# Unit 0's query low parts moved, the mixing product cut in four, an exact first block of the up projection, and the last tiles' evictions shared anew

## The chip, the cores and the metric

One core of a Trainium2 chip runs the whole program in one launch. The metric is the device time of an execution in microseconds (us). TensorE is called PE here, VectorE DVE, ScalarE ACT, GpSimd POOL, SyncE SP; SP issues all loads and stores of this kernel.

## The reference

`x` has 32 samples of 32 rows of 512 numbers. The block adds two branches to it:

```python
x = x + attn(cond(x, cond_128, ...), Wq, Wk, Wv, Wo, q_norm_w, k_norm_w)
x = x + ffn(cond2(x, cond_128, ...), gate_w, gate_z, gate_s, up_w, up_z, up_s, down_w, down_z, down_s)
...
def cond2(x, embedding, ...):          # 8 experts, one mixed 32x32 matrix a sample
    agg_w = einsum('bk,koi->boi', softmax(...), weight)
    return einsum('boi,bih->boh', agg_w, x) + agg_b[:, :, None]
def dequantize(w, s, z):               # groups of 128 rows; w and z are integers 0 to 15
    return (w - repeat(z, 128)) * repeat(s, 128)
def ffn(x):                            # 512 -> 1792 -> 512
    return (silu(x @ gate_proj) * (x @ up_proj)) @ down_proj
```

Attention has 32 query heads and 8 key/value heads of size 128, over the 32 rows of each sample, with RMS norm on queries and keys, a causal mask and a linear bias. The results are float32, so the kernel splits most operands into a high and a low 16-bit part and adds up three products (high by high, high by low, low by high).

## The kernel before, in words

The program is written by hand, engine by engine; a semaphore stands for each hand-over, and each engine works its list strictly in the order of the code. The work has four parts.

**Start.** A convolution gives the attention's input, the gates of the eight experts are computed, weights and inputs are scaled by powers of two. POOL multiplies the mixing matrices by the gates in one instruction (`mixing_products`, L1792, 2048 numbers a partition); DVE sums that product over the experts (`mixing_sums`, L1450).

**Attention** runs in 16 units, two halves of the tokens for each of 8 key/value heads. In unit 0, which has no unit in front of it to fill its waits, PE projects the queries, turns them (`transpose_q`, L676), turns the keys (`transpose_k`, L683), projects keys and values of unit 1 and computes the scores. ACT evicts a turned query block to `qhi` (L1086), DVE computes the low part `qlo` (`queries_low`, L1473). `transpose_k` waits for the second `qlo`, since it writes the same PSUM bank. In DVE's list the scaling of the output weights (`scale_wo`, L1364, 2048 numbers a partition, in SBUF) stands in front of the first two `queries_low`. Each later unit also prepares a part of the FFN's weights: `up_ints` (DVE, L1525) takes the zeros off, `up_scaled` (POOL) multiplies by the scales, `up_high` (ACT) and `up_low` (DVE, L1529) split the product into `uphi` and `uplo`, all four blocks of 128 rows at once. Gate and down weights stay exact integers (`gint`, `dints`), and their scales are applied when a product is evicted.

**FFN** has 28 tiles, 14 slices of the inner size for each half of the tokens. For tile n PE runs `gate(n)` (4 blocks, 2 matmuls each, L852 and L853), the first two blocks of `down(n-2)`, `up(n)` (4 blocks, 3 matmuls each, L539 to L541), and the last two blocks of `down(n-2)` (L888, L889; 2 matmuls each). ACT and DVE evict the gate blocks by turns into `whole` and `part` (L1213, L1689), POOL adds the two (`add_part`, L1905), ACT applies silu (L1218), DVE multiplies by the up product (`hidden`, L1695), ACT and POOL split the result into `hThi` and `hTlo` (L1224, L1911). DVE adds down blocks 0, 2 and 3 to `acc` (L1704); block 1 goes through ACT (L1236) and POOL (L1921). `whole` and `part` have two buffers, so ACT's eviction of gate block 0 of tile n waits for `hTlo` of tile n-2.

The first two tiles lie beside the last unit of the attention. DVE computes the scales of a half in `mix_scales` (L1676, L1677), between two steps that PE waits for.

**End.** After tile 27 PE runs `down(26)` and `down(27)`, then `turn_last` turns the second half's result back (L915), DVE adds it to `x` in four steps (`result`, L1717), and SP stores (L527).

Of the kernel before, what the change touches and what calls it, by code (L numbers as in the profile page):

```python
# [86 lines left out]
def build(nc, x_in, xt_in, mask_in, fs_in, cond_in, cw_in, conv_in, wq_in, wkv_in, wo_in, w0_in, w1_in, w2_in, b2_in, mix_in, vec_in,  # L87
          gu_w_in, gu_z_in, gu_s_in, up_s_in, dn_w_in, dn_z_in, dn_s_in, const_in, sel_in, out):
    ctx = ExitStack()
    with ctx:  # L90
# [83 lines left out]
        uplo = sb("uplo", [P, IC, KC, P], F16)  # L174
# [35 lines left out]
        rest = sb("rest", [P, DM - 2 * IC * KC - IC * KC - 2 * HQ - 10], F32, att)  # L210
# [31 lines left out]
        between = sb("between", [P, 7 * DM + 40], F32, ffn)  # L242
# [103 lines left out]
        d_gint = sem("d_gint")  # L346
        d_usub = sem("d_usub")
# [11 lines left out]
        d_fscl = sem("d_fscl")  # L359
        t_fT = sem("t_fT")  # L360
# [6 lines left out]
        a_silu = sem("a_silu")  # L367
        t_u = sem("t_u")
        d_h = sem("d_h")
# [6 lines left out]
        a_dn = sem("a_dn")  # L376
        p_acc = sem("p_acc")
# [26 lines left out]

        def turned_bank(half, c):

            return side if half else (PA[0], PA[1], PC[2], PC[3])[c]
# [9 lines left out]
        def down_bank(n, c):  # L417

            return bank[c] if n == TILES - 1 else PC[c % 2]
# [27 lines left out]
        def _(sp):  # L447
# [77 lines left out]
            for q in range(NQ):  # L525
                sp.wait_ge(d_res, q + 1)
                sp.dma_start(out[:, q, :], x[:, q, :]).then_inc(l_out, 16)  # L527
# [4 lines left out]
        def _(pe):  # L532
# [306 lines left out]
            def gate(n):  # L839
# [3 lines left out]
                for g in range(KC):  # L843
# [6 lines left out]
                    if g == 0 and n in (1, 2):  # L850
                        pe.wait_ge(d_h, n)
# [4 lines left out]
            def up(n):  # L856
# [3 lines left out]
                if n < 2:  # L860
                    pe.wait_ge(a_g, 2 * n + 1)
                elif n == 2:
                    pe.wait_ge(d_y, HQ * UNITS)
                else:
                    pe.wait_ge(d_h, n)
                split_product(up_bank(n)[:, :], [(uphi[:, i, c, :], uplo[:, i, c, :], fThi[:, c, tokens(half)],
                                                  fTlo[:, c, tokens(half)]) for c in range(KC)],
                              True, True).then_inc(t_u, 1)

            def down(n, blocks=range(KC)):  # L870
                last = n == TILES - 1
                pe.wait_ge(a_dtr, n + 1)
                if last:
                    pe.wait_ge(d_hlo, 1)
                else:
                    pe.wait_ge(p_hlo, n + 1)
                for c in blocks:
                    if last:
                        pe.wait_ge(d_g if c % 2 else a_g, 2 * TILES - 1 + c // 2)
                    elif c >= 2:  # L880
# [5 lines left out]
                    ints = dtr[:, n % 2, P * c:P * c + P]  # L886
                    o = down_bank(n, c)
                    mm(o[:, :], ints, hThi[:, n % (LAG + 1), :], start=True, stop=False)  # L888
                    mm(o[:, :], ints, hTlo[:, n % (LAG + 1), :], start=False, stop=True).then_inc(t_dn, 1)  # L889
# [13 lines left out]
            def turn_last():  # L903
# [3 lines left out]
                pe.wait_ge(d_res, HQ)  # L907
                pe.wait_ge(d_h, TILES)
                for c in (0, 2, 3, 1):
# [4 lines left out]
                    for t in range(HQ):  # L914
                        last = nc.tensor.transpose(PC[t][:, P * c:P * c + P], acc[:, 1, c, P * t:P * t + P], ident)  # L915
                        if c == 1:
                            last.then_inc(t_yT, 1)
# [41 lines left out]
            for n in range(TILES - LAG, TILES):  # L959
                down(n)  # L960
# [4 lines left out]
        def _(act):  # L965
# [108 lines left out]
            def up_high(i):  # L1074
                act.wait_ge(p_umul, i + 1)
                A(uphi[:, i, :, :], raw[:, 1, :].bitcast(F32).rearrange("p (c n) -> p c n", c=KC), ACT.Copy,
# [126 lines left out]
            def scaled(n, g):  # L1203
                half, i = divmod(n, IC)
                act.wait_ge(t_g, KC * n + g + 1)
                if i == 0 and g == 0:
                    act.wait_ge(d_fscl, half + 1)
# [11 lines left out]

            def hidden_high(n):  # L1220
                act.wait_ge(d_h, n + 1)
# [28 lines left out]
            outputs_high(UNITS - 1)  # L1250
            gate(0)
            hidden_high(0)
            mix_input(4)
            scaled(1, 0)
            scaled(1, 2)
            mix_input(5)
            gate(1)
            hidden_high(1)
            mix_input(6)
            act.wait_ge(d_dint, IC)  # L1260
# [3 lines left out]
            for n in range(2, TILES):  # L1264
# [16 lines left out]
                down_ints(n - 1)  # L1281
                gate(n)
# [3 lines left out]
            down_scaled(TILES - 1)  # L1286
# [3 lines left out]
        def _(dve):  # L1290
# [157 lines left out]
            def mixing_sums(h):  # L1448
                dve.wait_ge(p_mixp, 1)
# [73 lines left out]
            def up_ints(i):  # L1523
                dve.wait_ge(l_up, 48 * i + 48)
                V.tensor_tensor(raw[:, 1, :].bitcast(F32), raw[:, 1, :], zeros[:, 1, :], ALU.subtract).then_inc(d_usub, 1)  # L1525

            def up_low(i):
                dve.wait_ge(a_uphi, i + 1)
                V.scalar_tensor_tensor(uplo[:, i, :, :], raw[:, 1, :].bitcast(F32).rearrange("p (c n) -> p c n", c=KC),  # L1529
                                       upk[:, 0:1], uphi[:, i, :, :], ALU.mult, ALU.subtract).then_inc(d_uplo, 1)  # L1530
# [160 lines left out]
            def hidden(n):  # L1691
                dve.wait_ge(a_silu, n + 1)
                dve.wait_ge(t_u, n + 1)
# [311 lines left out]
```

## Time and profile before

| what | us |
| --- | --- |
| median of 3 runs (732.04 to 732.96) | 732.92 |
| the profiled execution | 738.87 |
| its span, first to last instruction | 737.1 |

The profile describes the one execution of 738.87 us. "Busy" is the time in which an engine had an instruction under way. Matmuls are pipelined: a record of one 512-column matmul is about 0.38 us long, while the next begins 0.216 us after it. The granted clock is 1.00 at the full 2.4 GHz and 0.50 at 1.2 GHz.

### The profile page before, as it was taken

To read this page: it belongs to the slowest core of one execution; us is meant where nothing else is said; L and a number is where in the kernel's file an instruction comes from. 1 tells how busy PE (TensorE), PEld (TensorE's weight loads), DVE (VectorE), ACT (ScalarE), POOL (GpSimd) and SP (SyncE) were. 2 spreads that over 40 slices of the span, in tenths; PEclk is the share of its full clock that TensorE was granted. 3 is DMA by queue.
4 is the path that set the end of the run, shared out by engine and by line. 5 is a ranking of instruction groups with operands and counts; after the bars stand their busy time and mean duration, and the time that the engine had idled before them with its cause. 6 is when DMAs were issued, how large, how long until landed. Compare 5 with 4: busy or idle time off the path is not lost.

```text
span 737.1 us, 14750 instructions
## 1 busy us (share of the span) xinstructions
PE 719.0 (98%) x5350; PEld 433.6 (59%) x5350; DVE 503.6 (68%) x764; ACT 438.2 (59%) x1293; POOL 420.6 (57%) x349
## 2 busy tenths in 40 slices
PE   9997999999999999999999999999899999999996
PEld 8755555656656566565665656656545555555554
DVE  5977777677666757666776775574655776666666
ACT  1475574845757576495575757647555665545553
POOL 0473974853766484485476648448334556646663
PEclk9998999999999999999999999999999999999999
DMA  8410242342331323234233121220000000010001
GB/s 267 189 40 1 102 144 73 116 157 71 114 128 57 117 93 103 71 114 153 75 113 129 57 93 64 73 72 30 1 1 1 0 1 2 0 44 16 0 1 58
DMA packets 21738, 54.20 MB, mean 74 GB/s; under 512 B 3744, under 2 KB 4288, under 8 KB 19520
## 3 DMA queue, kind: packets, MB, share of 16 engines
q1 hardware_dynamic: 21696, 53.67, 21.6%
q8 instruction: 22, 0.36, 0.2%
q14 instruction: 20, 0.16, 0.1%
HBM read 51.57 MB, written 2.10 MB: 73 GB/s over the span
## 4 chain that ended last, share of the span: by engine, by line
PE 87%; DVE 5%; POOL 5%; ACT 2%; issue 1%; DMA 1%; SPq 0%; DVEq 0%; ACTq 0%; POOLq 0%
PE bank L539 21%; PE bank L540 20%; PE bank L541 20%; PE bank L676 4%; PE bank L888 3%; PE bank L889 3%; PE bank L852 3%; PE bank L853 3%; PE bank L591 2%; PE bank L718 1%; POOL wqlo L1803 1%; PE bank L683 1%; PE bank L703 1%; PE bank L693 1%; PE bank L692 1%
## 5 line engine op out<-in xcount | busy, mean ns | idle before, releaser
L539 PE MATMUL bank<-wohi,oThi 128*128 128x512 f16 x256 | 97.2, 380 | 1.7 <-DVE oTlo L1507 1.6
L539 PE MATMUL bank<-wqhi,cThi 128*128 128x512 f16 x256 | 97.1, 379 | 1.2 <-POOL wqlo L1803 0.6
L540 PE MATMUL bank<-wolo,oThi 128*128 128x512 f16 x256 | 97.1, 379 | 0.0
L541 PE MATMUL bank<-wohi,oTlo 128*128 128x512 f16 x256 | 97.1, 379 | 0.0
L540 PE MATMUL bank<-wqlo,cThi 128*128 128x512 f16 x256 | 97.1, 379 | 0.0
L541 PE MATMUL bank<-wqhi,cTlo 128*128 128x512 f16 x256 | 97.1, 379 | 0.0
L1820 POOL TENSOR_TENSOR qinv<-qms,neghalf 128x8 f32<-128x8 f32 x32 | 52.7, 1646 | 46.4 <-ACT qms L1028 46.4
L1020 ACT ACTIVATE qsq<-qraw 128x128 f32<-128x128 f32 x256 | 75.8, 299 | 4.7
L1515 DVE SCALAR_TENSOR_TENSOR x<-bank,ysc,x 128x512 f32<-128x512 f32 x64 | 48.0, 750 | 42.2 <-PE bank L541 41.6
L1813 POOL TENSOR_TENSOR wolo<-wor,wohi 128x512 f16<-128x512 f32 x32 | 36.3, 1156 | 70.1 <-ACT wohi L991 70.1
L1911 POOL TENSOR_TENSOR hTlo<-whole,hThi 128x512 fp32r<-128x512 f32 x27 | 34.6, 1282 | 71.1 <-ACT hThi L1224 71.1
L1827 POOL TENSOR_TENSOR qn<-qraw,qinv 128x512 f32<-128x512 f32 x64 | 68.8, 1094 | 4.2 <-POOL qinv L1820 3.2
L539 PE MATMUL bank<-wkvhi,cThi 128*128 128x256 f16 x256 | 70.4, 275 | 0.0
L540 PE MATMUL bank<-wkvlo,cThi 128*128 128x256 f16 x256 | 70.3, 275 | 0.0
L541 PE MATMUL bank<-wkvhi,cTlo 128*128 128x256 f16 x256 | 70.2, 274 | 0.0
L1086 ACT ACTIVATE qhi<-bank 128x512 f16<-128x512 f32 x64 | 36.1, 590 | 46.7 <-PE bank L676 46.0
L1704 DVE SCALAR_TENSOR_TENSOR acc<-bank,dscl,acc 128x512 f32<-128x512 f32 x78 | 55.6, 742 | 0.5 <-PE bank L889 0.5
L888 PE MATMUL bank<-hThi,dtr 128*128 128x512 f32 x112 | 54.5, 486 | 1.0 <-ACT dtr L1229 0.7
L1803 POOL TENSOR_TENSOR wqlo<-wqr,wqhi 128x512 f16<-128x512 f32 x32 | 37.9, 1215 | 26.4 <-ACT wqhi L977 26.4
L1473 DVE TENSOR_TENSOR qlo<-bank,qhi 128x512 f16<-128x512 f32 x64 | 42.6, 686 | 12.2 <-ACT qhi L1086 12.2
L1507 DVE SCALAR_TENSOR_TENSOR oTlo<-bank,oThi 128x512 f16<-128x512 f32 x64 | 39.7, 684 | 15.2 <-ACT oThi L1112 15.2
L1695 DVE SCALAR_TENSOR_TENSOR whole<-bank,hc,whole 128x512 f32<-128x512 f32 x28 | 21.0, 751 | 40.8 <-PE bank L541 36.7
(194 smaller groups left out, 1884.5 us busy)
## 6 DMA issues: line engine op xcount, KB each, us to landing
wqr<-in_wq SPq DMA_DIRECT2D x8, 1024.0 KB, 4.8
wor<-in_wo SPq DMA_DIRECT2D x8, 1024.0 KB, 4.9
raw<-in_gu_w SPq DMA_DIRECT2D x28, 256.0 KB, 2.8
zeros<-in_gu_z SPq DMA_DIRECT2D x28, 256.0 KB, 3.6
wkvr<-in_wkv SPq DMA_DIRECT2D x8, 512.0 KB, 4.1
srow<-in_up_s SPq DMA_DIRECT2D x14, 256.0 KB, 4.1
raw<-in_dn_w SPq DMA_DIRECT2D x14, 256.0 KB, 3.2
zeros<-in_dn_z SPq DMA_DIRECT2D x14, 256.0 KB, 4.4
```

Source lines behind the costliest of these rows:

```text
L539: mm(o, ahi, bhi, start=start and k == 0, stop=False)
L540: mm(o, ahi, blo, start=False, stop=False)
L541: last = mm(o, alo, bhi, start=False, stop=stop and k == n - 1)
L888: mm(o[:, :], ints, hThi[:, n % (LAG + 1), :], start=True, stop=False)
L1020: A(qsq[:, t % 2, g, :], qraw[:, t, g, :], ACT.Square, accum_out=qss[:, t, g:g + 1]).then_inc(a_qss, 1)
L1473: V.tensor_tensor(qlo[:, BQ * t:BQ * t + BQ, :, :].rearrange("p b g s -> p g b s"), query_bank(u, t)[:, :].rearrange("p (g b s) -> p g b s ...
L1507: V.scalar_tensor_tensor(oTlo[:, :, :, b, :], PC[b][:, :].rearrange("p (t g s) -> p t g s", t=HQ, g=G), O_DOWN, oThi[:, :, :, b, :], ALU.m ...
L1515: V.scalar_tensor_tensor(x[:, q, :], PC[t][:, :], ysc[:, half:half + 1], x[:, q, :], ALU.mult, ALU.add).then_inc(d_y, 1)
L1704: V.scalar_tensor_tensor(o, down_bank(n, c)[:, :], dscl[:, i, c:c + 1], o, ALU.mult, ALU.add).then_inc(d_dn, 1)
L1803: Q.tensor_tensor(wqlo[:, c, :], wqr[:, c, :], wqhi[:, c, :], ALU.subtract).then_inc(p_wq, 1)
L1820: Q.tensor_tensor(qinv[:, pair, :], qms[:, pair, :], neghalf[:, pair, :], ALU.pow).then_inc(p_qpow, 1)
L1827: Q.tensor_tensor(qn[:, t, :, :], qraw[:, t, :, :], qinv[:, t, :, None].broadcast_to([P, G, HD]), ALU.mult).then_inc(p_qn, 1)
```

## The change

Four edits. (1) In DVE's list for unit 0 the first two `queries_low` stand in front of `scale_wo`, and the maximum over the second key/value weights stands behind `queries_low(0, 3)`. (2) `mixing_products` is four instructions of a quarter each. (3) Block 0 of the up weights stays integers: its two matmuls make a product of their own (PE list: one matmul less a tile), in bank PA[1] for tiles 0 and 1 and PA[0] after; ACT evicts it with its scale into a new tile `exact` (`up_exact`); DVE adds the other blocks' product to it (`up_sum`, in the place of `hidden`), POOL multiplies by the silu result (`hidden`, new on POOL; on DVE for the last tile), and POOL's and ACT's lists are put in another order. The preparation of the up weights works on three blocks; block 0 is one DVE subtraction. `mix_scales` has one instruction more, and its second call goes to ACT (`later_scales`). (4) At the end `down(26)` and `down(27)` use banks of their own, the order of DVE's list changes, and one of the four final additions goes through ACT and POOL, with a store issued by ACT.

```diff
@@ DVE, unit 0
             score_scale()
-            scale_wo()
             queries_low(0, 0)
             queries_low(0, 1)
-            link(weight_max(M_KV, wkvr, l_wkv, 1))
+            scale_wo()
             keys_low(0)
             queries_low(0, 2)
             queries_low(0, 3)
+            link(weight_max(M_KV, wkvr, l_wkv, 1))
             out_scale()
@@ POOL
-                Q.tensor_tensor(mixp[:, :, :, :], ..., ALU.mult).then_inc(p_mixp, 1)
+                for q in range(0, NQ, 2):
+                    Q.tensor_tensor(mixp[:, q:q + 2, :, :], ..., ALU.mult).then_inc(p_mixp, 1)
@@ PE, up(n)
                 if n < 2:
-                    pe.wait_ge(a_g, 2 * n + 1)
-                elif n == 2:
+                    pe.wait_ge(d_g, 2 * n + 1)
+                pe.wait_ge(a_g, 2 * n + 1)
+                o = exact_bank(n)[:, :]
+                mm(o, uphi[:, i, 0, :], fThi[:, 0, tokens(half)], start=True, stop=False)
+                mm(o, uphi[:, i, 0, :], fTlo[:, 0, tokens(half)], start=False, stop=True).then_inc(t_ue, 1)
+                if n == 2:
                     pe.wait_ge(d_y, HQ * UNITS)
-                else:
-                    pe.wait_ge(d_h, n)
-                split_product(up_bank(n)[:, :], [... for c in range(KC)],
+                elif n > 2:
+                    pe.wait_ge(d_us, n)
+                split_product(up_bank(n)[:, :], [... for c in range(1, KC)],
                               True, True).then_inc(t_u, 1)
@@ PE, last tiles
+            def last_downs():
+                n = TILES - 2
+                pe.wait_ge(a_dtr, n + 1)
+                pe.wait_ge(p_hlo, n + 1)
+                pe.wait_ge(d_res, HQ)
+                down_block(n, 0)
+                pe.wait_ge(d_us, TILES)
+                down_block(n, 1)
...
+                n = TILES - 1
+                pe.wait_ge(a_dtr, n + 1)
+                pe.wait_ge(d_hlo, 1)
+                down_block(n, 1)
...
@@ ACT
+            def up_exact(n):
+                half, i = divmod(n, IC)
+                act.wait_ge(t_ue, n + 1)
+                if n >= 2:
+                    act.wait_ge(p_h, n - 1)
+                A(exact[:, n % 2, :], exact_bank(n)[:, :], ACT.Copy, scale=uscl[:, half, i:i + 1]).then_inc(a_u, 1)
@@ ACT, tile n of the loop
-                if n > 2:
-                    hidden_high(n - 1)
                 scaled(n, 2)
+                hidden_high(n - 1)
                 if n >= LAG:
                     down_scaled(n - LAG)
+                up_exact(n)
@@ ACT, end
-            down_scaled(TILES - 1)
+            A(dprod[:, 1, :], down_bank(TILES - 1, 1)[:, :], ACT.Copy, ...).then_inc(a_dn, 1)
+            act.wait_ge(t_yT, HQ + 1)
+            A(fnat[:, 0, :], last_bank(0)[:, :], ACT.Copy).then_inc(a_yT, 1)
+            act.wait_ge(p_res, 1)
+            act.dma_start(out[:, HQ, :], x[:, HQ, :]).then_inc(l_out, 16)
@@ DVE
             def mix_scales(half):
...
+                link(V.tensor_scalar(uscl[:, half, :], gus[:, 1, :, 0], finv[:, column], None, ALU.mult))
...
+            def up_sum(n):
+                dve.wait_ge(a_u, n + 1)
+                dve.wait_ge(t_u, n + 1)
+                u = exact[:, n % 2, :]
+                V.scalar_tensor_tensor(u, up_bank(n)[:, :], hc[:, n // IC:n // IC + 1], u, ALU.mult,
+                                       ALU.add).then_inc(d_us, 1)
...
-                hidden(n)
+                up_sum(n)
+                if n == TILES - 1:
+                    last_hidden()
                 if n >= LAG:
                     down_added_to(n - LAG, 2)
-                if n == 7:
-                    mix_scales(1)
+            hidden_low(TILES - 1)
             down_added_to(TILES - 3, 3)
             down_added_to(TILES - 2, 0)
-            hidden_low(TILES - 1)
@@ POOL, tile n of the loop
                 if n > LAG:
-                    hidden_low(n - 1)
+                    hidden(n - 1)
+                    add_down(n - 1 - LAG)
                 add_part(n)
-                add_down(n - LAG)
+                hidden_low(n - 1)
+            pool.wait_ge(d_hlo, 1)
+            add_down(TILES - 1 - LAG)
             add_down(TILES - 2)
             add_down(TILES - 1)
+            pool.wait_ge(a_yT, 1)
+            Q.tensor_tensor(x[:, HQ, :], fnat[:, 0, :], x[:, HQ, :], ALU.add).then_inc(p_res, 1)
```

## Rows read from the trace of the kernel before

**Rows 1.** The page: the span, and PE's busy time, share and instructions

```profile
span 737.1 us, 14750 instructions
PE 719.0 (98%) x5350; PEld 433.6 (59%) x5350; DVE 503.6 (68%) x764; ACT 438.2 (59%) x1293; POOL 420.6 (57%) x349
```

**Rows 2.** Windows: stretch, length, busy us of each engine, granted clock, DMA

```profile
58.70:63.20 4.50, 4.49 (x21) 3.85 (x22) 3.38 (x6) 2.95 (x11) 0.00 (x0) 0.50 0.00 0
...
107.00:524.00 417.00, 416.89 (x3540) 252.99 (x3538) 278.40 (x416) 261.95 (x907) 251.96 (x216) 1.00 0.28 92
```

**Rows 3.** Waits of PE in 0 to 107 us: total us, times, longest

```profile
PE bank L683 <- DVE qlo L1473: 4.7, 1, 4.7
```

**Rows 4.** Timeline of DVE, units 0 and 12: start, us, line, operation, tiles

```profile
41.14 0.94 DVE L1444 TENSOR_TENSOR mixb<-le,vec 128x64 f32<-128x64 f32 x1
51.76 5.61 DVE L1364 TENSOR_SCALAR wor<-wor,wup 128x2048 f32<-128x2048 f32 x1
57.29 1.27 DVE L1473 TENSOR_TENSOR qlo<-bank,qhi 128x512 f16<-128x512 f32 x2
58.48 1.20 DVE L1336 TENSOR_REDUCE mx<-wkvr 128x1 f32<-128x1024 f32 x1
65.81 0.42 DVE L1462 SCALAR_TENSOR_TENSOR vlo<-bank,vhi 128x256 f16<-128x256 f32 x1 [2.57 <-ACT vhi L1044]
...
430.45 1.29 DVE L1364 TENSOR_SCALAR wor<-wor,wup 128x2048 f32<-128x2048 f32 x1
```

**Rows 5.** Timeline of POOL, unit 0

```profile
40.92 2.09 POOL L1827 TENSOR_TENSOR qn<-qraw,qinv 128x512 f32<-128x512 f32 x2
51.78 4.50 POOL L1792 TENSOR_TENSOR mixp<-mixw,le 128x2048 f32<-128x2048 f32 x1
```

**Rows 6.** Timelines of ACT and PE, unit 0

```profile
51.87 1.08 ACT L1086 ACTIVATE qhi<-bank 128x512 f16<-128x512 f32 x2 [0.72 <-DVE wn L1435]
53.59 0.38 PE L541 MATMUL bank<-wqhi,cTlo 128*128 128x512 f16 x1
61.29 0.42 PE L539 MATMUL bank<-wkvhi,cThi 128*128 128x256 f16 x1
```

**Rows 7.** The chain of work that ended last: start, us, what

```profile
67.79 1.05 POOL sc L1841
101.56 4.50 DMA srow<-in_up_s
540.87 0.39 PE bank L539
```

**Rows 8.** Timeline of PE over one tile of the FFN

```profile
687.05 0.39 PE L852 MATMUL bank<-fThi,gint 128*128 128x512 f16 x1
689.73 0.39 PE L539 MATMUL bank<-fThi,uphi 128*128 128x512 f16 x1
693.26 0.39 PE L852 MATMUL bank<-fThi,gint 128*128 128x512 f16 x1
```

**Rows 9.** Window over the same tile

```profile
687.05:693.26 6.21, 6.21 (x29) 3.31 (x29) 4.21 (x7) 3.62 (x6) 3.78 (x3) 1.00 0.00 1
```

**Rows 10.** Timelines of ACT and POOL over the same tile

```profile
687.70 0.69 ACT L1213 ACTIVATE whole<-bank,gscl 128x512 f32<-128x512 f32 x1 [1.58 <-PE bank L853]
691.71 0.63 ACT L1218 ACTIVATE whole<-whole 128x512 f32<-128x512 f32 x1 [0.59 <-POOL whole L1905]
...
690.41 1.27 POOL L1905 TENSOR_TENSOR whole<-whole,part 128x512 f32<-128x512 f32 x1 [0.15 <-DVE part L1689]
```

**Rows 11.** Timeline of DVE before the first tiles

```profile
533.38 0.25 DVE L1677 TENSOR_SCALAR gscl<-gus,finv 128x56 f32<-128x56 f32 x1
```

**Rows 12.** Timelines of PE and DVE at the end

```profile
718.14 0.39 PE L852 MATMUL bank<-fThi,gint 128*128 128x512 f16 x1
...
727.58 3.38 DVE L1704 SCALAR_TENSOR_TENSOR acc<-bank,dscl,acc 128x512 f32<-128x512 f32 x5 [0.23 <-PE bank L889]
731.82 2.48 DVE L1717 TENSOR_TENSOR x<-bank,x 128x512 f32<-128x512 f32 x4 [0.86 <-PE bank L915]
```

More of the change, by code:

```diff
@@ L241, in build @@
         hTlo = sb("hTlo", [P, LAG + 1, HT], F32R, ffn)
-        between = sb("between", [P, 7 * DM + 40], F32, ffn)
+        exact = sb("exact", [P, 2, HT], F32, ffn)
+        between = sb("between", [P, 5 * DM + 40], F32, ffn)
         dtr = sb("dtr", [P, 2, DM], F32R, ffn)
@@ L376, in build @@
         a_dn = sem("a_dn")
+        a_yT = sem("a_yT")
+        p_res = sem("p_res")
         p_acc = sem("p_acc")
@@ L860, in up, with down_block, down @@
                 if n < 2:
-                    pe.wait_ge(a_g, 2 * n + 1)
-                elif n == 2:
+                    pe.wait_ge(d_g, 2 * n + 1)
[4 more added lines that the diff above has]
+                if n == 2:
                     pe.wait_ge(d_y, HQ * UNITS)
-                else:
-                    pe.wait_ge(d_h, n)
-                split_product(up_bank(n)[:, :], [(uphi[:, i, c, :], uplo[:, i, c, :], fThi[:, c, tokens(half)],
-                                                  fTlo[:, c, tokens(half)]) for c in range(KC)],
+                elif n > 2:
+                    pe.wait_ge(d_us, n)
+                split_product(up_bank(n)[:, :], [(uphi[:, i, c, :], uplo[:, i, c - 1, :], fThi[:, c, tokens(half)],
+                                                  fTlo[:, c, tokens(half)]) for c in range(1, KC)],
                               True, True).then_inc(t_u, 1)
-            def down(n, blocks=range(KC)):
-                last = n == TILES - 1
+            def down_block(n, c):
+                ints = dtr[:, n % 2, P * c:P * c + P]
+                o = down_bank(n, c)[:, :]
+                mm(o, ints, hThi[:, n % (LAG + 1), :], start=True, stop=False)
+                mm(o, ints, hTlo[:, n % (LAG + 1), :], start=False, stop=True).then_inc(t_dn, 1)
+            def down(n, blocks):
                 pe.wait_ge(a_dtr, n + 1)
[L873 to L876, printed above, removed]
+                pe.wait_ge(p_hlo, n + 1)
                 for c in blocks:
-                    if last:
-                        pe.wait_ge(d_g if c % 2 else a_g, 2 * TILES - 1 + c // 2)
-                    elif c >= 2:
+                    if c >= 2:
                         pe.wait_ge(a_dn if c == 3 else d_dn, n + 1 if c == 3 else down_added(n, 0))
@@ L885, in down @@
                         pe.wait_ge(d_y, HQ * (UNITS - 1) + c + 1)
[L886 to L889, printed above, removed]
+                    down_block(n, c)
+            def last_downs():
+                n = TILES - 2
+                pe.wait_ge(a_dtr, n + 1)
+                pe.wait_ge(p_hlo, n + 1)
+                pe.wait_ge(d_res, HQ)
+                down_block(n, 0)
+                pe.wait_ge(d_us, TILES)
+                down_block(n, 1)
+                pe.wait_ge(a_g, 2 * TILES)
+                down_block(n, 2)
+                pe.wait_ge(d_g, 2 * TILES)
+                down_block(n, 3)
+                n = TILES - 1
+                pe.wait_ge(a_dtr, n + 1)
+                pe.wait_ge(d_hlo, 1)
+                down_block(n, 1)
+                pe.wait_ge(a_u, TILES)
+                down_block(n, 0)
+                pe.wait_ge(d_dn, down_added(n - 2, 3))
+                down_block(n, 2)
+                down_block(n, 3)
             def turn_back(half, q):
@@ L958, in _ @@
                     turn_back(0, 2 * n - 2 * IC - 2 * LAG + 1)
-            for n in range(TILES - LAG, TILES):
-                down(n)
+            last_downs()
             turn_last()
@@ L1734, in _ @@
             outputs_low(UNITS - 1)
-            hidden(0)
+            up_sum(0)
             up_low(IC - 1)
@@ L1740, in _ @@
             add_outputs(UNITS - 1, 1, 1)
-            hidden(1)
+            up_sum(1)
             add_outputs(UNITS - 1, 1, 2)
@@ L1779, in _ @@
                 down_added_to(TILES - 1, c)
-            for q in range(HQ, NQ):
+            for q in range(HQ + 1, NQ):
                 result(q)
@@ L1905, in add_part, with hidden @@
                 Q.tensor_tensor(whole[:, n % 2, :], whole[:, n % 2, :], part[:, n % 2, :], ALU.add).then_inc(p_whole, 1)
+            def hidden(n):
+                pool.wait_ge(d_us, n + 1)
+                pool.wait_ge(a_silu, n + 1)
+                Q.tensor_tensor(whole[:, n % 2, :], whole[:, n % 2, :], exact[:, n % 2, :], ALU.mult).then_inc(p_h, 1)
             def hidden_low(n):
@@ L1927, in _ @@
             add_part(0)
+            mix_low(4)
+            hidden(0)
+            mix_low(5)
+            add_part(1)
             hidden_low(0)
-            mix_low(4)
-            add_part(1)
-            mix_low(5)
-            hidden_low(1)
             mix_low(6)
+            hidden(1)
             mix_low(7)
```

91 lines of the change are left out of this document (61 added, 30 removed).

## The prediction

> **What bounds the kernel now.** I read the page first: PE is busy for 719.0 of 737.1 us [rows 1]. So a gain must come from fewer matmuls or from the few places where PE waits or runs slowly. The windows by stage say where these are. From 107 to 524 us, units 2 to 15, PE is busy for 416.89 of 417.00 us [rows 2]: nothing done to other engines there can gain. The table of waits names one long wait of PE ahead of 107 us, 4.7 us of the key transposes for `qlo` [rows 3]. A window behind it adds that from 58.70 to 63.20 us the granted clock was 0.50, the 1.2 GHz level, after that idle time [rows 2]. In the FFN one tile takes 693.26 - 687.05 = 6.21 us of unbroken matmuls [rows 8], while DVE is busy for 4.21, ACT for 3.62 and POOL for 3.78 us of it [rows 9]: PE sets the pace. The end is a serial stretch of evictions [rows 12].
>
> **Unit 0.** The wait comes from DVE's list. `scale_wo` began at 51.76 and took 5.61 us, against 1.29 us for the same instruction in unit 12; it ended 1.1 us after POOL's 4.50 us product, which ran from 51.78 to 56.28 [rows 4, 5]. So DVE stood behind POOL, and both `qlo` stood behind DVE. After the change the two `qhi` are there at 52.4 and 52.95 (from 51.87, 0.54 us each [rows 6]), and the two `qlo`, which read PSUM, take 0.6 us each [rows 4]: done at 53.7. PE's last matmul of the projection ends at 53.59 + 0.38 = 53.97 [rows 6], so the transposes start at once, 4.7 us earlier. At 61.29 the key and value matmuls began at the low clock [rows 6]. Without the idle time I expect no drop, since PE's work in front of it ran at full clock; 4.5 us of half-clock work becomes 2.25, a second gain of 2.25 us. That makes 6.95 for PE.
>
> DVE must keep up. `scale_wo` waits for a POOL instruction to end. With pieces of 4.50 / 4 = 1.13 us the next end is at 54.0, so it runs to 55.3. Then `klo` and two `qlo` of about 0.65 us to 57.3, the maximum moved behind them, 1.20 us [rows 4], to 58.5, two small scalings of some 0.45 us together, and `vlo` starts at 58.95 instead of 65.81 [rows 4]: 6.8 us earlier. DVE, not PE, sets the shift, and POOL's step at 67.79, which follows from `vlo` over the scores, moves with it [rows 7]. From there to 107 us the chain runs through POOL, a load of 4.50 us issued after POOL's step, and PE [rows 7]; each is released by the one in front, so all shift alike. **Gain 6.8 us**; bounds 4.5 (DVE does not get in between the pieces, below) and 6.95.
>
> That DVE gets in rests on `mixb`: two POOL instructions followed each other from 40.92 for 2.09 us; `mixb`, issued at 41.14, ended at 42.08, just behind the first of them [rows 4, 5]. The waiting engine was let in at the boundary. The delayed pieces of the product cost nothing: they end at 57.6, POOL has nothing to do before its step at 67.79 - 6.8 = 61.0 [rows 7], and DVE reads them later still.
>
> **Up weights in units 2 to 15 and the head of the FFN.** One more DVE instruction and shorter DVE, POOL and ACT work per slice: nothing, hidden behind PE (416.89 of 417.00 busy [rows 2]). If the cover were gone the small DVE instruction would cost about 0.1 us each time, 14 times.
>
> **FFN tiles.** PE runs 28 matmuls less, 29 - 1 per tile. From 687.05 to 689.73 lie twelve matmuls, 0.223 us each; the f16 ones alone step by 0.216 (the section on the profile has it), and I take that. In tile 0 it gains nothing, since PE then waits for `oTlo` until 540.87 [rows 7]. Tiles 1 to 27: 27 x 0.216 = **5.8 us**, if no new wait appears. Bounds 0 and 6.05.
>
> So I walk through the new tile of 6.0 us, from its first gate matmul, with durations of [rows 9, 10]. ACT: gate block 0 from 0.65 (687.70 - 687.05), block 2 to 2.15, `hThi` to 2.75, down block 1 to 3.45, the new `up_exact` (0.69 us long, 0.59 from start to start) to 4.05, `dtr` to 4.6, silu to 5.2 (before: 691.71 + 0.63, that is 5.3). In sum 3.62 + 0.6 = 4.2 of 6.0 us. DVE: no instruction more, 4.21. POOL: four instead of three instructions of 1.27 us, 5.1 of 6.0 us: the new product waits for `up_sum` of the tile before at 0.1 and ends at 1.35, `add_down` 2.6, `add_part`, which needs both DVE gate evictions, from 3.0 to 4.25, `hTlo` to 5.5. PE's own new wait, gate block 0 evicted before the exact block enters its bank, ends at 1.25, needed at 2.7. The next gate block 0 waits for `up_exact`, 4.05, needed at 6.0. `hTlo` at 5.5 is needed by ACT at 6.65. Every wait ends over 0.6 us early.
>
> **Scales ahead of the first tiles.** `uscl` is one more linked DVE instruction between two low parts that PE needs; its neighbour takes 0.25 [rows 11]. PE's step at 540.87 [rows 7] comes **0.2 us later**; bounds 0 and 0.3. In half 1 the same work moves to ACT, beside PE's matmuls: nothing, or some 0.8 us once if tile 7 had no slack.
>
> **The end.** Measured from tile 27's first gate matmul, 718.14 [rows 12], the span ends after 18.96 us. The new banks let `down(26)` follow at once, so `hThi` and `hTlo` of tile 27 set `down(27)` at about 8.1 us. DVE still adds seven blocks behind that, at 3.38 / 5 = 0.68 us [rows 12]: to 12.9 us, where the last one ended at 730.96, 12.8, before. The last steps shrink: four additions in 2.48 us [rows 12] become three, 0.6 us less, with the fourth over ACT (0.69) and POOL (1.27 [rows 10]) in parallel, 2.0 us against 1.9. The new store from ACT's queue starts no later than SP's last. Together 0.6 us less, of which 0.2 is tile 27's matmul, counted above: **gain 0.4 us**; bounds -1.0 (POOL's branch and its store end last) and 1.5.
>
> **Sum.** 6.8 + 5.8 - 0.2 + 0.4 = 12.8 us. Against the profiled execution, 738.87 us, this gives 726.1. The median of the runs shown is 732.92, 0.8% lower; no term scales enough for that to matter, so I predict 732.92 - 12.8 = **720.1 us**.
>
> **The rivals.**
> *DVE is not let in between the pieces.* POOL's four pieces follow each other, and `scale_wo` waits until about 56.4. Then `vlo` starts 58.95 + 2.3 = 61.25, the gain in unit 0 is 4.5, and the time is 722.4. `mixb` speaks against it, though it is one case with another DVE instruction. The Trainium skill, page "SBUF — State Buffer", section "SBUF: two separate sides", says that DVE and GpSimd share a port pair as an exclusive lock: whoever starts first holds it for the whole instruction and the other fully blocks. By that rule the 5.61 us [rows 4] are explained, but nothing promises the waiting side the next turn, and the time would be this rival's 722.4.
> *The clock still falls.* If the low clock comes anyway, 2.25 us are lost: 722.4 too. Against it: the idle time in front of it is gone.
> *The matmul saved is waited away.* A hand-over in the new order ends last in each tile and the tile stays at 6.21: 5.8 less gain, 725.9. The slack of 0.6 us on POOL is the thinnest.
> *Slower: the ring over two buffers of `whole`.* From gate block 0's eviction at 0.65 to `hTlo` of the same tile at 6.0 + 5.5 is 10.85 us, and it must fit in two tiles. The other gains are 7.0 us; spread over 26 tiles that is 0.27, so it decides from a tile of 6.48, a ring of 12.96. If each of POOL's four steps were held up by a DVE instruction of 0.74 us, the ring would be 13.8, a tile 6.9, and the time 732.92 - 7.0 + 26 x 0.69 = 744. Against it: DVE's FFN instructions read PSUM, and beside them POOL's 1.27 us do not vary.
> *A gain that isn't there.* Unit 0's shift is taken back before 107 us by something that I didn't see, and the tiles gain nothing: about 732.5.
>
> **Chances.** Forecast 0.70; either of the two at 722.4 0.13; 725.9 0.10; slower 0.03; no gain 0.04, of which half counts as small gains. A measurement of this kernel can tell 0.2%, 1.5 us, from no change: faster 0.95, same 0.02, slower 0.03. The low end takes the upper bounds of unit 0 and the end, 720.1 - 0.15 - 1.1 and some tenths for an execution's spread: 718.3. The high end takes in 722.4 with the lower bound of the end: 723.6. Outside lie 725.9 and what is worse, 0.17.
>
> **What would show it.** In the changed profile: `scale_wo` about 1.3 us long from 54; no wait of 4.7 us at `transpose_k`, clock 1.00 from 54 to 66; `vlo` at 59; the first PE-bound stretch from 100 us; a tile of 6.0 us in the FFN, with POOL busy for 5.1; the span's end 18.4 us after tile 27's first matmul. The forecast is wrong if a tile takes over 6.1 us, or if the clock is below 1 after 54 us.

## The result, and the profile after

| | before | after |
|---|---|---|
| median of the timed runs | 732.48 us (731.84 to 732.96) | 727.98 us (727.12 to 728.39, 4 runs) |
| the profiled execution | 738.87 us | 728.39 us |
| its span | 737.1 us | 725.1 us |
| its mean granted clock | 0.994 | 0.999 |

The ratio of the times is 0.9938, 95% interval 0.9920 to 0.9955: faster by 4.5 us, where 12.8 were forecast, and 4.4 us above the high end of the range. The two spans differ by 12.0 us. So the traces show nearly the gain that was predicted, and the runs do not. That is the question of this case.

The page and the windows of the kernel after; the first window is unit 0 behind the evictions of the queries, the second one FFN tile (stretch, length, then busy us of PE, PEld, DVE, ACT, POOL with instructions, the granted clock, DMA):

```profile
span 725.1 us, 14838 instructions
PE 709.9 (98%) x5322; PEld 429.3 (59%) x5322; DVE 497.4 (69%) x777; ACT 453.3 (63%) x1325; POOL 452.4 (62%) x380
...
53.00:66.00 13.00, 12.50 (x121) 8.43 (x120) 11.30 (x17) 10.43 (x39) 10.03 (x9) 1.00 0.00 1
700.23:706.23 6.00, 6.00 (x28) 3.21 (x28) 4.24 (x7) 4.19 (x7) 5.05 (x4) 1.00 0.00 0
```

PE has 28 matmuls less than in [rows 1]. The tile is 6.00 us long against the 6.21 of [rows 9], with all of it PE's, and unit 0 runs at full clock. The same stretch of the kernel before:

```profile
53.00:66.00 13.00, 8.26 (x88) 6.74 (x87) 9.31 (x10) 5.91 (x26) 3.28 (x1) 0.74 0.00 0
```

88 matmuls instead of 121, at a mean clock of 0.74. Unit 0 of the kernel after, timelines of DVE and POOL:

```profile
51.02 0.16 DVE L1505 TENSOR_TENSOR wn<-wcol 128x1 f32<-128x1 f32 x1
51.92 1.29 DVE L1543 TENSOR_TENSOR qlo<-bank,qhi 128x512 f16<-128x512 f32 x2 [0.73 <-ACT qhi L1132]
53.12 1.28 DVE L1434 TENSOR_SCALAR wor<-wor,wup 128x2048 f32<-128x2048 f32 x1
59.08 0.42 DVE L1532 SCALAR_TENSOR_TENSOR vlo<-bank,vhi 128x256 f16<-128x256 f32 x1
...
51.02 1.07 POOL L1916 TENSOR_TENSOR kn<-kraw,kinv 128x512 f32<-128x512 f32 x1
52.06 5.94 POOL L1872 TENSOR_TENSOR mixp<-mixw,le 128x512 f32<-128x512 f32 x4
```

`scale_wo` (`wor`) fits between two pieces of the product: 1.28 us instead of 5.61, and the four pieces take 5.94 where the whole took 4.50 [rows 4, 5]. `vlo` starts at 59.08, was 65.81. PE's wait of 4.7 us for `qlo` is gone. The seam before the first tiles and the last tile, from PE's and DVE's timelines:

```profile
526.70 0.24 DVE L1749 TENSOR_SCALAR uscl<-gus,finv 128x14 f32<-128x14 f32 x1
534.46 0.39 PE L561 MATMUL bank<-wohi,oThi 128*128 128x512 f16 x1 [0.74 <-DVE oTlo L1577]
706.23 0.39 PE L876 MATMUL bank<-fThi,gint 128*128 128x512 f16 x1
712.36 0.69 DVE L1775 TENSOR_TENSOR whole<-whole,exact 128x512 f32<-128x512 f32 x1
714.36 4.70 DVE L1783 SCALAR_TENSOR_TENSOR acc<-bank,dscl,acc 128x512 f32<-128x512 f32 x7
719.80 1.88 DVE L1796 TENSOR_TENSOR x<-bank,x 128x512 f32<-128x512 f32 x3 [0.74 <-PE bank L962]
```

Read against [rows 7, 12]: PE's step in front of the tiles moves from 540.87 to 534.46, 6.4 us. Tile 27 begins at 706.23 instead of 718.14, 11.9 us; so the FFN gave 5.5. Behind it the end takes 725.1 - 706.23 = 18.87 us against 18.96.

### The profile page after: what moved, and what is told of

It reads as the page before. It is cut to its first block, busy times and chain, and to the rows that moved or that the text cites. A ratio compares the mean times of both kernels' runs of the same rounds, so it can differ in the third digit from the quotient of the medians.

```text
span 725.1 us, 14838 instructions
## 1 busy us (share of the span) xinstructions
PE 709.9 (98%) x5322; PEld 429.3 (59%) x5322; DVE 497.4 (69%) x777; ACT 453.3 (63%) x1325; POOL 452.4 (62%) x380
## 4 chain that ended last, share of the span: by engine, by line
PE 86%; POOL 5%; DVE 4%; DMA 2%; issue 1%; SPq 1%; ACT 1%; DVEq 0%; POOLq 0%
PE bank L561 20%; PE bank L563 20%; PE bank L562 20%; PE bank L698 3%; PE bank L901 3%; PE bank L902 3%; PE bank L876 3%; PE bank L877 3%; PE bank L740 2%; POOL wqlo L1883 1%; DMA xT<-in_xt 1%; PE bank L888 1%; PE bank L705 1%; PE bank L889 1%; PE bank L725 1%
## 5 line engine op out<-in xcount | busy, mean ns | idle before, releaser
L1543 DVE TENSOR_TENSOR qlo<-bank,qhi 128x512 f16<-128x512 f32 x64 | 42.4, 685 | 12.8 <-ACT qhi L1132 12.8
L1986 POOL TENSOR_TENSOR whole<-whole,part 128x512 f32<-128x512 f32 x28 | 35.5, 1270 | 24.9 <-DVE part L1762 24.9
L1066 ACT ACTIVATION_READ_ACCUMULATOR qsq<-qraw 128x1 f32 x256 | 48.4, 189 | 0.0
```

The lines of the kernel that those rows point to most:

```text
L1066: A(qsq[:, t % 2, g, :], qraw[:, t, g, :], ACT.Square, accum_out=qss[:, t, g:g + 1]).then_inc(a_qss, 1)
L1543: V.tensor_tensor(qlo[:, BQ * t:BQ * t + BQ, :, :].rearrange("p b g s -> p g b s"), query_bank(u, t)[:, :].rearrange("p (g b s) -> p g b s ...
```

## The experiments

All times are medians of timed runs, beside runs of the kernel before on the same chip; "traced" means the profiled execution of that kernel.

### Is the profiled execution of before like its timed runs?

**e1_before_again** is the kernel before, unchanged; **e7_after_again** the kernel after, unchanged.

> The kernel of before, unchanged, timed and profiled once more. Theory A (an order that is decided anew in each execution): whether DVE's scaling of the output weights or POOL's mixing product gets going first in unit 0 differs from execution to execution; the timed runs at 732.5 us are those where DVE is first, the profiled one at 738.87 us one where it lost. Then a new profile shows either a scaling of 1.3 us and a span of 729 to 731 us, or one of 5.6 us and 737 us, and the timed median stays at 732.5. Theory B (the stall is in every execution, and the profiled execution was slower for another reason): the scaling takes 5.6 us again and the span is 737 us, while the timed runs stay at 732.5.

Measured: the traced execution took 738.83 us, and the eleven others of this label 732.06 to 732.86; the 27 runs beside it 731.71 to 733.80, median 732.6. The spans of the others are 730.2 to 731.0 us, the traced one's 736.9. So one program has two times, 6.2 us apart, and both of its two traces so far caught the longer one. DVE and POOL in the traced execution:

```profile
51.26 1.05 DVE L1435 TENSOR_TENSOR wn<-wcol 128x1 f32<-128x1 f32 x1
52.23 5.61 DVE L1364 TENSOR_SCALAR wor<-wor,wup 128x2048 f32<-128x2048 f32 x1
...
51.25 1.04 POOL L1836 TENSOR_TENSOR kn<-kraw,kinv 128x512 f32<-128x512 f32 x1
52.25 4.51 POOL L1792 TENSOR_TENSOR mixp<-mixw,le 128x2048 f32<-128x2048 f32 x1
```

> The changed kernel, unchanged, timed beside the others. It is 5.7 us below before in span and was 4.5 below in time. If what lies outside the span belongs to the change (a store on ACT's queue): time minus span is 3.3 again and the time 728.0. If it belonged to those runs alone: time minus span is 2.1, as in the kernel without the unit 0 edits, and the time 727.4.

Measured: 727.49 us (726.96 to 728.57), ratio 0.9927 [0.9913, 0.9940]. All nine timed runs of the kernel after so far lie between 726.96 and 728.57: it has one time.

### Each part of the change by itself

**e2_unit0_alone**: the kernel before with the new order in unit 0 and the product in four pieces.

```diff
-                dve.wait_ge(p_mixp, 1)
+                dve.wait_ge(p_mixp, 2 * h + 2)
...
-            scale_wo()
             queries_low(0, 0)
             queries_low(0, 1)
-            link(weight_max(M_KV, wkvr, l_wkv, 1))
+            scale_wo()
             keys_low(0)
             queries_low(0, 2)
             queries_low(0, 3)
+            link(weight_max(M_KV, wkvr, l_wkv, 1))
...
+                for q in range(0, NQ, 2):
+                    Q.tensor_tensor(mixp[:, q:q + 2, :, :], ...)
```

> Only the moved query low parts and the mixing product in four pieces, on the kernel of before. Theory A: the timed runs of before mostly lack the stall, so the time is 732.5 us, within 1 us; the profile shows no wait of 4.7 us and a span of about 730 us. Theory B: the edit takes 6.8 us off every execution, 725.7 us.

Measured: 732.35 us, ratio 0.9998 [0.9989, 1.0007]. **e3_unit0_undone** takes the same lines out of the kernel after.

> The changed kernel with the two unit 0 edits undone. Theory A: the time is that of the changed kernel, 728.0 us within 1 us, in runs where DVE is first; the exact block and the end alone give the 4.5 us. Theory B: 728.0 + 6.8 = 734.8 us.

Measured: 727.54 us, ratio 0.9932 [0.9919, 0.9946], against 727.49 with them (e7). Unit 0's edits are worth 0.0 to 0.3 us in timed runs, from both sides. The trace of e3 is the first to show the old list without the stall:

```profile
51.25 0.16 DVE L1505 TENSOR_TENSOR wn<-wcol 128x1 f32<-128x1 f32 x1
51.33 2.07 DVE L1434 TENSOR_SCALAR wor<-wor,wup 128x2048 f32<-128x2048 f32 x1
...
51.26 1.06 POOL L1915 TENSOR_TENSOR kn<-kraw,kinv 128x512 f32<-128x512 f32 x1
52.28 5.51 POOL L1871 TENSOR_TENSOR mixp<-mixw,le 128x2048 f32<-128x2048 f32 x1
```

This is what to compare with e1, line by line. Here `wn`, a product of one number per partition, takes 0.16 us; `scale_wo` is then issued while `kn` runs, gets in behind it and is done at 53.40; POOL's product pays, 5.51 instead of 4.50. In e1 `wn` takes 1.05 us and ends with `kn`. `scale_wo` and the product are then recorded 0.02 us apart, at 52.23 and 52.25; that the product was in front is read from the durations, 5.61 against 4.51. The first trace of before has the same pair, at which I had not looked:

```profile
50.78 1.05 DVE L1435 TENSOR_TENSOR wn<-wcol 128x1 f32<-128x1 f32 x1
...
50.78 1.04 POOL L1836 TENSOR_TENSOR kn<-kraw,kinv 128x512 f32<-128x512 f32 x1
```

What gives `wn` 0.16 or 1.05 us is finer than these hundredths. The trace of e2 has the starts of e1, and the short `wn`:

```profile
51.26 0.16 DVE L1435 TENSOR_TENSOR wn<-wcol 128x1 f32<-128x1 f32 x1
...
51.25 1.07 POOL L1837 TENSOR_TENSOR kn<-kraw,kinv 128x512 f32<-128x512 f32 x1
```

In nanoseconds, over all traces in which nothing was put in front of `wn`, its record starts from 9 ahead of `kn`'s to 4 behind it in the ten with the short `wn`, and 5 to 7 behind it in the three with the long one (before, e1 and e14). So "who comes first" below is inferred from this order: `kn`'s record may start up to 4 ns ahead and `wn` is still not held up.

**e8_end_undone** keeps the exact block and takes the end back: the old banks, the order of the last low part and additions, the last eviction by DVE, all stores by SP.

```diff
-            hidden_low(TILES - 1)
             down_added_to(TILES - 3, 3)
             down_added_to(TILES - 2, 0)
+            hidden_low(TILES - 1)
...
-            for q in range(HQ + 1, NQ):
+            for q in range(HQ, NQ):
                 result(q)
...
-            pool.wait_ge(d_hlo, 1)
             add_down(TILES - 1 - LAG)
```

> The changed kernel with the end put back: banks, orders of DVE and PE, four final additions on DVE, all stores by SP. By the prediction's term the new end is worth 0.4 us, so 0.4 above the changed kernel. By the traces (the stretch from tile 27's first matmul to the end was 18.96 before and is 18.87 now, one matmul of 0.22 less included): 0 to 0.2 us below the changed kernel in span, and 0.3 more below it in time if the ACT store costs that outside the span.

Measured: 729.50 us (728.81 to 730.38), ratio 0.9950 [0.9937, 0.9964]: 3.3 us for the exact block, and 2.0 for the new end. DVE, POOL and PE of e8 in the last tile, and the windows around the wait:

```profile
712.74 1.33 DVE L1755 TENSOR_TENSOR whole<-whole,exact 128x512 f32<-128x512 f32 x1
...
712.23 1.30 POOL L1987 TENSOR_TENSOR acc<-acc,dprod 128x512 f32<-128x512 f32 x1
...
714.88 0.77 PE L897 MATMUL bank<-hThi,dtr 128*128 128x512 f32 x1 [2.10 <-DVE acc L1763]
...
712.80:714.85 2.05, 0.00 (x0) 0.00 (x0) 2.05 (x3) 1.26 (x2) 0.73 (x1) 1.00 0.00 0
714.85:718.20 3.35, 3.32 (x7) 2.16 (x8) 1.91 (x4) 0.69 (x1) 0.47 (x1) 0.50 0.00 0
```

The exact block turns the last tile's product from an instruction that reads a bank into one with two inputs in SBUF. DVE's list has one instruction more there: the sum into `exact` takes the 0.75 us that `hidden` took before, and the product comes on top. With the old end the product meets POOL's addition and takes 1.33 us instead of 0.69; PE waits 2.1 us, where it waited 0.72 at the same place of the kernel before, and the granted clock behind that idle time is 0.50, the 1.2 GHz level, for 3.35 us. From tile 27's first matmul (706.63) to the end it is 21.1 us. The new end makes POOL wait for `d_hlo` and fills PE's gap with `down(26)`: 18.87. So the new end removes what the exact block would cost there.

### What decides between the two times of before?

My theory after e1 to e3 was: whoever comes first of `wn` and `kn`. The rival was that the moment at which `scale_wo` is issued decides.

**e4_scale_late**: three linked memsets of one number ahead of `scale_wo`, to bring it behind `kn`'s end.

```diff
             score_scale()
+            for _ in range(3):
+                link(V.memset(rowmax[:, :], 0.0))
             scale_wo()
```

> The kernel of before with three tiny DVE memsets in front of the scaling in unit 0, so that POOL's mixing product is always under way first. Theory A: every execution has the stall: 738 to 739 us, 6 us above before, scaling of 5 to 5.6 us in the profile, granted clock 0.5 for some us behind it. Theory B: before has it already, so the time stays at 732.5 us.

Measured: 732.81 us, ratio 1.0002 [0.9993, 1.0011]; the expected stall did not come, also not in the trace:

```profile
51.94 1.68 DVE L1364 TENSOR_SCALAR wor<-wor,wup 128x2048 f32<-128x2048 f32 x1
...
52.50 5.51 POOL L1794 TENSOR_TENSOR mixp<-mixw,le 128x2048 f32<-128x2048 f32 x1
```

The memsets were too short: `scale_wo` was issued at 51.94, `kn` ended at 52.54. A delay of 0.6 us inside `kn` costs nothing. That it is the side of `kn`'s end that counts is tested by the runs that follow.

**e5_stall_forced** puts DVE behind the product for certain: a first piece of an eighth, DVE waits for it, then come seven eighths. **e6_stall_forced_moved** adds the new order of DVE's list, with the wait still ahead of `scale_wo`.

```diff
             score_scale()
+            dve.wait_ge(p_mixp, 1)
             scale_wo()
...
+                for part_q in (slice(0, 1), slice(1, NQ)):
```

> The kernel of before, with the mixing product in two pieces (one eighth, then seven eighths) and DVE's scaling in unit 0 waiting for the first piece, so that POOL's long piece (about 3.9 us) is always under way before the scaling can start. Theory A (the stall is absent from the timed runs of before; its price is what the profiled execution showed): 738.8 us, 6.2 above before, in all timed runs, with the scaling over 4 us long and the clock at 0.5 behind the wait. Theory C (the stall is in the timed runs too, or costs nothing outside a profile): 732.6 us.

Measured: 739.42 us (738.96 to 740.26), ratio 1.0090 [1.0077, 1.0104]. The stall costs 6.6 us in timed runs too. In the trace `wn` took 0.16 us and `scale_wo`, issued behind the first piece, 4.97. So theory and rival are two links of one chain: the stall comes when `scale_wo` is issued too late to be ahead of the product, and a `wn` that is held up is what makes it late in the kernel before.

> The same forced order, with the query low parts moved in front of the scaling as in the change, the product still in two pieces. If moving alone is enough: 732.6 us. By the prediction's rival, where DVE is not let in between the pieces: the key low part waits for the scaling, about 57.5 us, and some 2 us of the stall stay: 734.5 us.

Measured: 735.92 us, ratio 1.0034 [1.0021, 1.0048]. PE's waits of `qlo` in e5 and in e6:

```profile
PE bank L683 <- DVE qlo L1473: 4.9, 1, 4.9
```

```profile
PE bank L691 <- DVE qlo L1473: 1.7, 1, 1.7
```

The order alone recovers 3.5 of 6.6 us: `scale_wo` is still held, 4.68 us, and now the last two `qlo`, for which the scores wait, stand behind it. That the pieces recover the rest is not shown by a pair of runs that differ in the pieces alone; e10 and e14, with both edits, have the order that stalls and no such wait.

**e9_wn_behind_kn** and **e10_after_wn_behind_kn** force the order of `wn` and `kn` in the kernels before and after.

```diff
+                dve.wait_ge(p_kn, 1)
                 V.tensor_tensor(wn[:, :], wcol[:, 0:1], wcol[:, 3:4], ALU.mult).then_inc(d_wn, 1)
```

> The kernel of before, where one tiny DVE instruction (wn, one number a partition) waits for POOL's kn, which normally starts within some 10 ns of it; nothing else is changed. Theory A, with its detail: which of the two is first decides all. With wn first, DVE's scaling is already waiting when kn ends and gets in ahead of the mixing product; with kn first, the product is under way when the scaling is issued. So 738.8 to 739.4 us in all timed runs. Rival: the order of these two doesn't matter, the product has to be issued early for another reason: 732.6 us.

Measured: 739.56 us (738.87 to 740.07), ratio 1.0091 [1.0076, 1.0107]. DVE of e9:

```profile
51.82 4.37 DVE L1436 TENSOR_TENSOR wn<-wcol 128x1 f32<-128x1 f32 x1 [1.18 <-POOL kn L1837]
56.12 1.28 DVE L1364 TENSOR_SCALAR wor<-wor,wup 128x2048 f32<-128x2048 f32 x1
```

One product of 128 numbers took 4.37 us beside POOL's 4.50, and `scale_wo` behind it its usual 1.28.

> The same added wait in the changed kernel. If the two unit 0 edits take the decision out of chance, the time stays at 727.5 us, at most 0.5 above; so the change would be worth 12 us in this order of the two, and 5 in the other.

Measured: 729.58 us (728.20 to 730.14), ratio 0.9951 [0.9935, 0.9967]. That is 2.1 above e7, where I expected at most 0.5. The spans, mostly 726.1 to 726.5 us against 724.8 to 725.4 in e7, account for 1.2 of it: PE waits 1.2 us of a `qlo`, as `wn` had to wait for the first piece of the product, and `scale_wo` took 1.65 us between two others. The rest lies outside the span, where three of these six runs have over 3 us (see "Outside the span" below). In this order the change is worth 739.56 - 729.58 = 10.0 us.

**e13_wn_a_little_later** touches nothing but a moment: one linked memset of one number, 0.06 us, ahead of `wn`.

```diff
+                link(V.memset(rowmax[:, :], 0.0))
                 V.tensor_tensor(wn[:, :], wcol[:, 0:1], wcol[:, 3:4], ALU.mult).then_inc(d_wn, 1)
```

> The kernel of before with one DVE memset of one number a partition, some 0.1 to 0.15 us, in front of wn, and no added wait on POOL. Theory A: wn and kn start within 10 ns of each other, so this is enough to put wn behind kn: 738.8 to 739.5 us in all timed runs. Rival: the two are further apart in the timed runs than in a trace, and the order holds: 732.7 us.

Measured: 738.79 us, all twelve runs from 738.10 to 739.74; ratio 1.0056 [1.0027, 1.0084]. DVE and POOL:

```profile
51.06 0.93 DVE L1436 TENSOR_TENSOR wn<-wcol 128x1 f32<-128x1 f32 x1
51.91 5.61 DVE L1364 TENSOR_SCALAR wor<-wor,wup 128x2048 f32<-128x2048 f32 x1
...
50.93 1.04 POOL L1837 TENSOR_TENSOR kn<-kraw,kinv 128x512 f32<-128x512 f32 x1
51.93 4.50 POOL L1793 TENSOR_TENSOR mixp<-mixw,le 128x2048 f32<-128x2048 f32 x1
```

With a memset of 0.06 us, which puts the start of `wn` 0.13 us behind that of `kn`, the kernel before is 6 us slower in every run. The ratio is smaller than the 1.0083 of the medians (738.79 over 732.74), and its interval wide, because of the 18 runs of before beside it 5 took 738.4 to 739.9 us, with spans of 736.6 to 738.1, and one 735.84: here, without being traced, the unchanged kernel fell on the long side as well. Of the 62 timed runs of it before this job none had; one, also at 735.84, lay between.

### What is left to gain at the end and at the seam

**e11_store_by_sp**: the kernel after, with the last store issued by SP instead of ACT.

```diff
+            sp.wait_ge(p_res, 1)
+            sp.dma_start(out[:, HQ, :], x[:, HQ, :]).then_inc(l_out, 16)
...
-            act.wait_ge(p_res, 1)
-            act.dma_start(out[:, HQ, :], x[:, HQ, :]).then_inc(l_out, 16)
```

> The changed kernel, with the last store issued by SP behind the three others instead of by ACT. Time minus span was 1.8 in all runs of before and of kernels without that store, 2.1 to 3.5 with it. If ACT's store is the cause: 1.8 again, the span the same or 0.3 longer (the issue comes behind three others), 727.2 us. If it is not: 2.1 or more stays, 727.5 us or above.

Measured: 727.12 us, ratio 0.9924 [0.9907, 0.9941], beside 727.49 of e7 in another job: 0.4 less, not distinct. Time minus span was 1.95 to 2.2 us in five runs and 3.4 in one, so it did not go back to 1.8.

**e12_scales_later** (e11 with the scales behind PE's needs, `up_scales` last) and **e14_scales_in_gap** (all three together in DVE's gap); in both ACT waits for the scales ahead of its first `up_exact`:

```diff
             turned_low(0, 0)
-            mix_scales(0)
             turned_low(0, 1)
...
             turned_low(0, 3)
+            mix_scales(0)
             scaled(0, 1)
             scaled(0, 3)
+            up_scales()
```

> As the kernel with the store by SP, and the three small DVE scalings ahead of the first tiles moved: the gate scales behind the fourth low part, the other two behind the second gate eviction. If the chain through the low parts sets PE's next step there, as the prediction took it, 0.5 to 0.7 us less: 726.6 us. If other waits hold it: 727.2 us.

Measured: 728.03 us, ratio 0.9940 [0.9924, 0.9956]: 0.9 slower than e11. DVE and PE of e12:

```profile
531.62 1.22 DVE L1754 TENSOR_SCALAR uscl<-gus,finv 128x14 f32<-128x14 f32 x1
...
535.28 0.39 PE L563 MATMUL bank<-wohi,oThi 128*128 128x512 f16 x1 [1.84 <-DVE oTlo L1579]
```

> As the kernel with the scales moved, but the other two small scalings directly behind the gate scales, where DVE sat idle for 0.9 us, and ahead of POOL's first addition, which held one of them up for a microsecond. If the scales' place in DVE's list is what the 0.3 us ahead of the first tiles hang on: the step of PE that waited at 534.4 comes 0.4 to 0.6 us earlier and the time is 0.5 below the kernel with the store by SP, 726.6 us. If not: 727.1 us.

Measured: 726.79 us (725.63 to 728.12), ratio 0.9901 [0.9864, 0.9938]; the runs of before beside it include the long ones. The same two places in e14:

```profile
528.94 0.23 DVE L1754 TENSOR_SCALAR uscl<-gus,finv 128x14 f32<-128x14 f32 x1
...
533.52 0.39 PE L563 MATMUL bank<-wohi,oThi 128*128 128x512 f16 x1 [0.47 <-DVE oTlo L1579]
```

In e12, behind `scaled(0, 3)`, the 14 numbers of `uscl` met a POOL addition and took 1.22 us for 0.24, and PE's step came at 535.28; in the gap, 533.52. The whole trace of e14 runs early, though: 0.49 us of its 0.94 ahead of the kernel after are there before this seam. Counted from DVE's `sc` in front of it, PE's step comes after 14.16 us in the kernel after, 15.09 in e12 and 13.71 in e14, so the place gives 0.45, as expected. This is the lowest median of the study, 0.7 below e7, but across jobs and within the spread of single runs.

The trace of e14 also settles what e10 could only force. By itself it fell into the order that stalls the kernel before, and its span is the shortest of all traces, 724.1 us:

```profile
50.55 1.05 DVE L1507 TENSOR_TENSOR wn<-wcol 128x1 f32<-128x1 f32 x1
53.46 1.66 DVE L1436 TENSOR_SCALAR wor<-wor,wup 128x2048 f32<-128x2048 f32 x1
```

`wn` was held up for 0.9 us and `scale_wo` for 0.4, no wait of PE for `qlo` appeared, and the granted clock stayed at 1.00 behind it. As far as this one execution shows, with both unit 0 edits it no longer matters which order comes about.

## Why the prediction was wrong

**The failed step is "Sum".** I saw that the median of the runs, 732.92, was 0.8% below the profiled execution, 738.87, and wrote that no term scales enough for that to matter. Nothing scales: the 6 us are one event. The 4.7 us wait of [rows 3] and the low clock of [rows 2] are in the traced execution; the timed runs that I predicted for did not have them (times of 732.0 to 733.0, and in e1 spans of 730.2 to 731.0 without the stall against 736.9 with it). I took 6.8 us off a time that did not contain them. Forced into all runs the stall costs 6.6 to 6.9 us (e5, e9) or 6.1 (e13), and the difference that I passed over was 5.95. Subtracting from 738.87 and reading the rest against 732.92 should have raised the question of which of the terms the timed runs have. Without unit 0 the same steps give 5.8 - 0.2 + 0.4 = 6.0 us, or 726.9; measured were 4.5 and, in e7, 5.4 (732.84 - 727.49). The range didn't cover this case either; and its high end, by its own terms, would have been 722.4 + 1.4 = 723.8, not 723.6.

**Unit 0.** For the execution that stalls the steps held. `scale_wo` began at 53.12, at the end of the first piece, and took 1.28 us (I had it wait for the second, to 54.0), `vlo` at 59.08 (58.95), the clock 1.00, PE's step in front of the tiles 6.41 earlier, that is 6.7 with the 0.27 of the scales added back (6.8); counted from `kn`'s start, which comes 0.24 later in the trace of after, it is 6.9. The rival "the clock still falls" is refuted by those rows. "DVE is not let in" is refuted by e10 and e14, where `scale_wo` did have to wait and took 1.65 us; in the trace of after it came just at a piece's end. For a timed run of before the term is 0.0 to 0.3 (e2, e3). What I had wrong in the mechanism is who decides: not the product's length, but `wn` against `kn`, 1.0 us ahead of `scale_wo`. The pair `wn`, `kn` at 50.78 with 1.05 and 1.04 us could have raised the question, since the instruction in front of `wn` in the same trace, also on one number per partition, took 0.15 us. The Trainium skill, page "SBUF — State Buffer", section "SBUF: two separate sides", counts DVE instructions with two inputs in SBUF among those that need the shared ports against a GpSimd one, and lets whoever starts first keep them to its end. The traces agree, 4.37 us for a `wn` of 0.16. The rule does not say who is next: in e3, e4, e10 and e14 a DVE instruction that was already issued got in between two POOL instructions that followed each other, so the hold until 56.4, from which I had 722.4, did not come.

**FFN tiles.** 6.21 to 6.00 us per tile as said; over the stretch 5.5 (from 177.27 to 171.77 us between PE's step and tile 27) against 26 x 0.216 = 5.6. POOL was busy for 5.05 us of the tile (5.1). "The matmul saved is waited away" and "the ring over two buffers" are refuted by the same rows.

**Scales ahead of the first tiles.** 0.27 us (0.2): PE's shift is 6.68 at DVE's `sc` in front of it (526.98 to 520.30) and 6.41 behind it. e12 and e14 show that it is the place that costs, not the instruction.

**The end.** 0.09 us in the traces, where 0.6 with the last matmul was said (18.4 us to the span's end; it was 18.87), and the reason was wrong: I compared the new end with the old one as it stood in the kernel before. With the exact block the old end is 21.1 us long (e8), so the new end is worth 2.0 and the exact block alone 3.3 in the timed runs; neither is 5.8 and 0.4. DVE's seven additions ended at 719.06, 12.83 us behind tile 27's first matmul, as forecast (12.9).

**Outside the span.** The spans of timed runs fell from 730.2 to 731.0 down to 724.5 to 725.1, about 5.8 us, close to the 6.0 of the remaining terms; the times fell by 4.5 to 5.4. For kernels with the old FFN time minus span is 1.75 to 1.95 us. With the exact block it is mostly 1.8 to 2.3, but in 13 of 44 runs 2.7 to 3.6: three of the four first runs of after, one of five in e7, three of six in e10, and, where SP issues all stores, two of five in e8, one of six in e11, two of six in e12 and one of seven in e14. So ACT's store is not needed for it, and I have no cause for it. It is why the times of the first four runs fell by less than their spans.

**Still open.** Why no job showed the full stall in 62 timed runs and then one showed it in 5 of 18, on the same chip as the job before it; why both traced executions of the unchanged kernel had it, while those of e2, e3 and e4 did not; and what the two runs at 735.84 were. That a shift of `wn` by little more than 0.1 us decides is shown by e13, and the traces with either `wn` lie within 16 ns of each other; what moves the two against each other is not known.

## What to carry to other kernels

Before a wait in a trace is priced, compare the profiled execution's time with the timed median: if they differ by about what the wait costs, ask first whether the timed runs have it, and look for the two instructions whose order it hangs on. Where DVE and POOL both work from SBUF and start within tens of ns, a tiny DVE instruction can hold a whole list up. Here the cure that was measured is to put what PE needs ahead of the long scaling and POOL's long work in pieces; it was worth nothing in the usual order and in the other made the change worth 10.0 us (e9, e10) instead of 5.4 (e7). A wait that keeps POOL's `kn` behind `wn` would be simpler, and no run tried it. An edit that moves a product from PSUM to SBUF is priced at the end of the kernel too, where no matmuls cover it.

## What the runs showed of the hardware that I had not expected

Two instructions that start within 10 ns of each other give one program two times, 732.6 and 738.8 us. A DVE instruction of 128 numbers took 4.37 us beside a POOL instruction of 4.50, and one of 14 per partition 1.22 instead of 0.24. In e3 and e4 a DVE instruction that waited was served before POOL's next one, and then it was POOL's that stretched, 4.50 to 5.51; in e10 and e14 a piece of 1.27 us became 2.25. Behind 2.05 us without matmuls in e8 the granted clock was 0.50 for the next 3.35 us.
